# A two-layer cross-attention and FFN kernel: the second attention's slot reordered, so that maxima and scores of the next batch stand in one stretch

## The reference, cut to what matters

```python
q = (Q @ Wq_w + Wq_b).reshape(b, tq, 16, 8); k, v likewise from the context
scores = einsum('bhqd,bhkd->bhqk', q, k) / sqrt(8)
scores = where(mask == 0, -1e9, scores)
attn = softmax(scores, axis=-1)
out = einsum('bhqk,bhkd->bhqd', attn, v) @ Wo_w + Wo_b
x = x + out                      # the residual
```

## The kernel before, in words

| j = 0 | j = 1 |
|---|---|
| transposes of the next pair (L1884, L1886) | |
| scores(b), turn_out(b-1), folds(b) | scores(b), turn_out(b-1), folds(b) |
| out_projection(b-1), score_maxima(b+1) | out_projection(b-1), score_maxima(b+1) |
| ffn_turn (L1999), queries_keys (L1893, L1894) | values_rows (L1901, L1902) |
| values(b), ffn_project (L2006) | values(b), in every fourth slot four transposes for the last FFN (L395) |
| turn_maxima(b+1) | turn_maxima(b+1) |

## Time and profile before

### The profile page before, as it was taken

How to read it: one execution, slowest core, us unless ns; L and a number is a source line. 1 busy time by engine, 2 the same in 40 slices (tenths; PEclk the granted TensorE clock), 3 DMA queues, 4 the chain that set the end, 5 groups by cost and what they waited for, 6 DMA issues and landing times.

```text
span 716.7 us, 23519 instructions
## 1 busy us (share of the span) xinstructions
PE 680.4 (95%) x9268; PEld 569.8 (80%) x9273; DVE 556.9 (78%) x1635; ACT 388.7 (54%) x846; POOL 432.1 (60%) x558
## 2 busy tenths in 40 slices
PE   8999999999999999999999989999999999998875
PEld 6788888888888888889888878788888888875544
DVE  5887787697687698688687655787878887778996
ACT  2443553543544544445345444566766766766896
POOL 3597586487396388378477523455555646632775
PEclk9999999999999999999999999999999999998999
DMA  9511011101101101101100120000000000000011
GB/s 263 132 34 37 13 48 45 33 5 46 37 26 45 36 2 45 36 26 36 36 22 15 32 79 7 11 7 7 12 5 4 9 4 9 0 2 1 24 45 52
DMA packets 26766, 23.82 MB, mean 33 GB/s; under 512 B 7148, under 2 KB 23356, under 8 KB 26680
## 3 DMA queue, kind: packets, MB, share of 16 engines
q1 hardware_dynamic: 25864, 22.25, 11.1%
q10 hardware_dynamic: 816, 0.36, 0.2%
HBM read 10.25 MB, written 2.10 MB: 17 GB/s over the span
## 4 chain that ended last, share of the span: by engine, by line
PE 70%; DVE 17%; POOL 5%; issue 4%; ACT 3%; DMA 1%; SPq 0%; ACTq 0%; DVEq 0%
PE bank L1274 7%; PE bank L1316 6%; PE bank L1942 6%; PE bank L1172 5%; PE bank L1296 4%; PE bank L1975 4%; PE bank L1278 4%; PE bank L1307 3%; PE bank L1173 3%; PE bank L1174 3%; DVE a_am L911 3%; PE bank L1960 2%; DVE f_h_max L2192 2%; PE bank L1223 2%; PE bank L1232 2%
## 5 line engine op out<-in xcount | busy, mean ns | idle before, releaser
L741 POOL TENSOR_TENSOR a_turned<-a_turned,a_rope 128x512 f32<-128x512 f32 x63 | 81.7, 1297 | 55.7 <-DVE a_turned L848 55.7
L742 POOL TENSOR_TENSOR a_qr<-a_straight,a_turned 128x512 f32<-128x512 f32 x64 | 81.6, 1276 | 4.9
L845 DVE TENSOR_TENSOR a_straight<-bank,a_rope 128x512 f32<-128x512 f32 x63 | 43.0, 683 | 52.5 <-PE bank L1174 51.4
L1045 ACT CAST a_qb<-a_qr 128x512 bf16<-128x512 f32 x64 | 39.8, 622 | 65.9 <-POOL a_qr L742 65.9
L1296 PE MATMUL bank<-a_vs,a_probs 77*64 77x65 f32 x2048 | 66.8, 222 | 0.0
L1296 PEld LDWEIGHTS bank<-a_vs,a_probs 77*64 77x64 f32 x2048 | 62.6, 137 | 3.3
L753 POOL TENSOR_TENSOR a_k_turned<-a_k_turned,a_rope 128x308 f32<-128x308 f32 x61 | 48.4, 793 | 24.3 <-DVE a_k_turned L858 23.6
L1316 PE MATMUL bank<-a_wo,a_oTn 128*128 128x128 f32 x512 | 62.6, 275 | 0.2 <-ACT a_oTn L1073 0.2
L1316 PEld LDWEIGHTS bank<-a_wo,a_oTn 128*128 128x128 f32 x512 | 60.5, 192 | 1.2 <-ACT a_oTn L1073 0.5
L911 DVE TENSOR_REDUCE a_am<-bank 128x6 bf16<-128x462 f32 (+1 forms) x96 | 49.9, 576 | 12.1 <-PE bank L1232 12.0
L1274 PE MATMUL bank<-a_qr,a_kr 64*77 64x128 f32 x960 | 59.2, 273 | 0.0
(11 more groups left out here) (282 smaller groups left out, 1984.8 us busy)
## 6 DMA issues: line engine op xcount, KB each, us to landing
a_vs<-a_stage SPq DMA_DIRECT2D x16, 312.8 KB
out<-x_all SPq DMA_DIRECT2D x16, 128.0 KB, 1.8
x_all<-in_x_dram SPq DMA_DIRECT2D x7, 256.0 KB, 6.3
a_vs<-a_stage SPq DMA_DIRECT2D x4, 308.8 KB
a_mask_in<-in_mask SPq DMA_DIRECT2D x16, 77.0 KB, 5.7
a_wv<-in_ctx SPq DMA_DIRECT2D x16, 77.0 KB
a_ctx_in<-in_ctx SPq DMA_DIRECT2D x8, 128.0 KB
a_vs<-a_stage SPq DMA_DIRECT2D x4, 211.2 KB
```

The source lines that it names most:

```text
L741: steps.link(nc.gpsimd.tensor_tensor(tv, tv, rope[:, 1:2, :].broadcast_to([128, 4, S]), ALU.mult))
L742: nc.gpsimd.tensor_tensor(qr[P][:, 2 * k:2 * k + 2, :, :].rearrange("p t j s -> p (t j) s"), sv, tv, ALU.subtract if made else ALU.add).th ...
```

## The change

TensorE: scores(b+1) are made behind score_maxima(b+1) in the slot of b, ahead of values(b), instead of at the head of the next slot. Their ten matmuls are in a new order, with a wait in the middle on a new semaphore `rest_read`, which VectorE raises when it has reduced the rest of the maxima. values_rows stands ahead of the folds, turn_out behind them, queries_keys ahead of out_projection; out_projection is no longer inside score_maxima. ffn_turn and ffn_project go from j = 0 to the slot j = 1. VectorE: the rest is reduced first; the attention's statistics (j = 1) and start.rows (j = 0) go behind the residual, directly ahead of the maxima; normalised_rows goes behind the maxima. ScalarE: turned_out goes behind the exponentials of the first group, ffn_turned to j = 1 ahead of cast_keys.

```diff
@@ VectorE
         def maxima(b):
+            dve.wait_ge(x_full[2], b + 1)
+            nc.vector.tensor_reduce(max_r[:], pr[:, 0:256].rearrange("p (h k) -> p h k", k=RPAD), AX,
+                                    ALU.max).then_inc(rest_read, 1)
             for i in (1, 0):
                 dve.wait_ge(x_full[i], b + 1)
                 steps.did(nc.vector.tensor_reduce(max_m[:, 8 * i:8 * i + 8],
                                                   px[i][:].rearrange("p (h k) -> p h k", k=KM), AX, ALU.max))
-            dve.wait_ge(x_full[2], b + 1)
-            steps.link(nc.vector.tensor_reduce(max_r[:], pr[:, 0:256].rearrange("p (h k) -> p h k", k=RPAD), AX, ALU.max))
+            steps.wait()
+            dve.wait_ge(rest_read, b + 1)
             nc.vector.tensor_tensor(row_max, max_m[:], max_r[:], ALU.max).then_inc(maxima_ready, 1)
...
-            if j == 1 and more_pre(p):
-                ffn_residual(p + 2)
-                statistics(p + 2)
...
-            if j == 0 and more_pre(p):
-                start.rows(dve, steps, p + 2)
...
+            if j == 1 and more_pre(p):
+                ffn_residual(p + 2)
             if not first:
                 dve.wait_ge(bias_added, p + j)
                 residual(b - 1)
             if j == 1 and more_pre(p):
-                normalised_rows(p + 2)
+                statistics(p + 2)
+            if j == 0 and more_pre(p):
+                start.rows(dve, steps, p + 2)
             if turn(P, j, g, 1):
                 front.variances(steps)
             if j == 0 or more:
                 maxima(b + 1)
+            if j == 1 and more_pre(p):
+                normalised_rows(p + 2)
@@ ScalarE
             if j == 1 and more:
+                if more_pre(p):
+                    ffn_turned(p + 2)
                 cast_keys(p + 1, 1 - P, 0)
+            exps(b, (2,))
             if not first:
                 turned_out(b - 1)
-            exps(b)
+            exps(b, (0, 1))
             if j == 0:
-                if more_pre(p):
-                    ffn_turned(p + 2)
@@ TensorE
         def scores(b, P, j):
...
-            score(2, 0, 0, 4, True).then_inc(half_done, 1)
-            for i in range(3):
+            for i in range(2):
                 score(1, i, 1, i, i == 0)
                 score(0, i, 0, i, i == 0)
+            score(1, 2, 1, 2, False)
+            pe.wait_ge(rest_read, b + 1)
+            score(2, 0, 0, 4, True).then_inc(half_done, 1)
+            score(1, 3, 1, 3, False)
+            score(0, 2, 0, 2, False)
             pe.wait_ge(half_done, 2 * b + 2)
             score(2, 1, 1, 4, False)
             score(0, 3, 0, 3, False)
-            score(1, 3, 1, 3, False)
...
         turn_maxima(0)
+        scores(0, 0, 0)
         def slot(b, p, P, j, more, g, prev):
             if j == 0 and more:
                 transposes(p + 1, 1 - P)
-            scores(b, P, j)
-            if not first:
-                turn_out(b - 1)
-            folds(b)
-            score_maxima(b + 1, ...)        # out_projection(b - 1) inside; ffn_turn behind it for j == 0
+            if j == 1 and more:
+                if more_pre(p):
+                    ffn_turn(p + 2)
+                values_rows(p + 1)
+            folds(b)
+            if not first:
+                turn_out(b - 1)
             if j == 0 and more:
                 queries_keys(p + 1)
-            if j == 1 and more:
-                values_rows(p + 1)
+            if j == 1 and more_pre(p):
+                ffn_project(p + 2)
+            if not first:
+                out_projection(b - 1)
+            score_maxima(b + 1, ...)
+            scores(b + 1, ...)
             values(b, p, P, j)
             if back(P, j, prev):
                 front.rows(pe, prev, pm)
-            if j == 0 and more_pre(p):
-                ffn_project(p + 2)
             if j == 0 or more:
                 turn_maxima(b + 1)
```

More of the change, by code:

```diff
@@ L1475, in layer1_attention @@
     m_full, fold_ready, maxima_ready, half_done = sem("m_full"), sem("fold_ready"), sem("maxima_ready"), sem("half_done")
+    rest_read = sem("rest_read")
     vals_ready = sem("vals_ready")
@@ L1765, in slot @@
                 queries(p + 1, 1 - P)
-        pairs_loop(dve, slot, steps, 56)
+        pairs_loop(dve, slot, steps, 52)
         normalise(B - 1)
@@ L1806, in fold_in, with exps @@
             nc.scalar.copy(fold[CROW:FOLD, :], MAXIMA[CROW:FOLD, :]).then_inc(fold_ready, 1)
-        def exps(b):
-            for g in (2, 0, 1):
+        def exps(b, gs):
+            for g in gs:
                 act.wait_ge(s_full[g], b + 1)
@@ L1904, in values_rows, with score_maxima @@
             last.then_inc(values_full, 1)
-        def score_maxima(b, p, P, j, first):
+        def score_maxima(b, p, P, j):
             pe.wait_ge(maxima_ready, b)
-            if not first:
-                out_projection(b - 2)
             pe.wait_ge(s_free[2], b)
@@ L2033, in tensor @@
         pe.wait_ge(setup, 11)
-        score_maxima(0, 0, 0, 0, True)
+        score_maxima(0, 0, 0, 0)
         yield
         turn_maxima(0)
+        scores(0, 0, 0)
         def slot(b, p, P, j, more, g, prev):
@@ L2041, in slot @@
                 transposes(p + 1, 1 - P)
-            scores(b, P, j)
+            if j == 1 and more:
+                if pair(p, 1):
+                    pe.wait_ge(front.means_read, 1)
+                if more_pre(p):
+                    ffn_turn(p + 2)
+                values_rows(p + 1)
+            folds(b)
             if not first:
                 turn_out(b - 1)
-            folds(b)
[L2046 to L2053, removed]
-            if j == 0 and more_pre(p):
-                ffn_turn(p + 2)
             if j == 0 and more:
                 queries_keys(p + 1)
-            if j == 1 and more:
-                values_rows(p + 1)
+            if j == 1 and more_pre(p):
+                ffn_project(p + 2)
+            if not first:
+                out_projection(b - 1)
+            if j == 0:
+                score_maxima(b + 1, p, P, 1)
+                scores(b + 1, P, 1)
+            elif more:
+                score_maxima(b + 1, p + 1, 1 - P, 0)
+                scores(b + 1, 1 - P, 0)
             if pair(p, PAIRS - 1) and j == 0:
```

## The result

| | before | after |
|---|---|---|
| median of 4 runs, us | 718.45 | 729.23 (728.61 to 730.0) |
| ratio, 95% interval | | 1.0145 (1.0131 to 1.0159) |
| span of the profiled execution | 716.7 | 727.3 |

The change costs 10.6 us of span. The direction of the forecast was right, the size half: +5.2, 723.3, and the range ended at 729. The page's line of after answers to the earlier trace rows: TensorE is busy 5.1 us longer with the same work. Its records are longer than the steps between them, so a short wait stands inside busy time, and half of the 10.6 us doesn't show as idle time.

A forecast was written before the change was run, and what follows sets the result against it. TensorE's own program, busy 95% of the span, was taken as the bound. Loop turns +2.5, rows_in +3.9, prologue -0.9 and the last pairs -0.3 gave +5.2 us on 718.1, so 723.3, range 715 to 729.

The forecast's parts named there:

- T to T: One slot, between starts of turn_maxima: forecast 6.12 us (j = 0) or 6.83 (j = 1).
- The prologue's term: In the prologue scores(0) moves into TensorE's wait for normalised_rows(1): -0.9 us once.
- R to V: From TensorE's semaphore for the reduced rest to values: 0.86 us, three pairs of halves, one weight load and exit.
- T to O: From turn_maxima's start to out_projection's: 2.03 us (j = 0), 2.44 (j = 1).
- O to V: From out_projection's start to values': 1.90+0.86 us (j = 0), 2.20+0.86 (j = 1).
- The wait for the rest in mid-scores: New TensorE wait on VectorE amid the scores: about 0.5 us for j = 1, 0.1 to 0.3 for j = 0.
- R: TensorE's semaphore for the reduced rest: 1.90 us behind out_projection's start (j = 0), 2.20 (j = 1).
- rows_in: Folds wait for ScalarE's fold copy queued behind rows_in: 0.65 us in each of six slots, +3.9.
- the end's sum: Last two pairs: no statistics or start.rows, but turned_out is awaited; about -0.3 us.
- The rival that the changes of shape win: Three of seven tile-shape changes go per slot; without waits for the rest 707 us; chance 0.16.
- possible form of this rival: Semaphore 1.82 us behind out_projection's start everywhere, no exposed weight load: four slots 25.2 us, total 715.

The follow-up runs named there:

- x11: After without the attention's statistics in slots j = 1 (two bn_stats, memset, two bn_aggr left out): 725.01 us.
- x12: x9 with start.rows behind the maxima and, on POOL, ffn_bias behind spread_keys: 726.78 us.
- x3: After with four scores instead of five ahead of the wait on rest_read, and (2, 1) last: 730.51 us.
- x2: After with ScalarE's copy of the next batch's fold ahead of rows_in: 727.87 us.
- b3: Before with values_rows behind values for j = 1, and transposes behind turn_out for j = 0: 726.97 us.
- y2: Before with only values_rows moved behind values for j = 1: 730.34 us.
- y3: x9 without the attention's statistics and without 120 of 128 columns of start.rows: 724.3 us.
- y1: x9 with the wait on rest_read two scores later: 725.62 us.
- x8: x1 with, for j = 1, turn_out ahead of the folds and ScalarE's turned_out ahead of the exponentials: 724.8 us.
- x9: x8, x2 and x4 together: 724.05 us.
- x1: After with ffn_project ahead of the folds for j = 1, and VectorE's ffn_residual and statistics ahead of the residual: 732.95 us.
- x4: After with VectorE's front.gather at the end of its slot instead of ahead of the residual: 730.89 us.

## Why the prediction was right in direction and short in size

Growth of the stage in stretches of slots, forecast and measured, both from T to T:

| slots | forecast | measured |
|---|---|---|
| 0 to 3 | -0.54 | +1.2 |
| 4 to 7 | +0.36 | +0.5 |
| 8 to 11 | +0.36 | +1.2 |
| 12 to 27, four turns | 4 x 1.01 = +4.0 | 4 x 1.59 = +6.3 |
| 28 to the end | +1.0 | +1.35 |

The stage grew by 5.4 us more than forecast. The prologue's term is 1.6 of it, R to V 1.7, T to O about 1.1 and a late VectorE in slot 8 0.5, each told below; the rest is spread over the end.

**Right: what decides O to V.** The wait for the rest in mid-scores, late for j = 1 because of the statistics, is shown by x11. R for j = 1 was forecast at O+2.2 and came at O+2.26 (the (2, 0) record at 513.92), for j = 0 at O+1.80 where 1.90 stood. O to V for j = 0 is 2.76 as summed, by luck: the 0.10 here makes up for the 0.10 that the next step missed. x12 shows that for j = 0 it is the floor and not start.rows, which the forecast blamed for 0.08.

**Mis-sized: R to V, 0.86.** It took one exposed load of weights. The half_done wait in the same stretch has a second: (2, 0) and (2, 1) use different halves of the array and one bank, and the second waits for the first (in x3, with four scores between them, R to V is 0.96 too). R to V is 0.96 to 0.97, inside the bounds of 0 and 0.2 that stood there for one load; that there are two was not counted. The 14 slots j = 1 have O to V 3.11 to 3.22 instead of 3.06, 1.7 us together.

**Mis-sized: T to O.** 2.03 to 2.09 against 2.03 for plain j = 0, 2.72 against 2.68 behind rows_in (together about 0.5 us), 2.41 against 2.44 for j = 1, but 2.58 in four slots with L395, 0.6 us. Those four are the slots behind a held combination: `queries` end 0.34 behind T there, and values_rows, which wait for them, start at T+0.44 instead of T+0.33. The sum had no term for GpSimd holding up VectorE.

**Right, for the wrong price: rows_in.** Forecast T to O 2.68, measured 2.72. But as a cause it was overvalued: x2 takes the wait away and gets 1.4 us of the 3.9, since the copies behind it on ScalarE were the next bound. Two prices for one delay don't add up, and the last interval of a slot (7.18 to 6.52) alone gave 0.66.

**Wrong: the prologue, -0.9.** scores(0) did move into the hole ahead of L1884; the folds stand 2.03 behind the first turn_maxima instead of 2.78 before. But slot 0 then makes scores(1) as well, and its length stays 7.52 (7.56 before). The sum took both the filled hole and the steady slot's saving of the scores at its head, for the same 1.3 us; they come back only behind the last turn_maxima, where no scores are left. This is the largest miss: the sum had slot 0 shorter by 0.76 (a steady slot j = 0) and 0.9, and it is shorter by 0.04, which is 1.6 of the 1.8 us missed in slots 0 to 3. Slot 1 is long (7.35 against 6.90 of slot 3), but was so before (6.33 against 5.94). Left out of the end's sum, that return hid what its waits cost: from 653.88 on, TensorE waits 1.01 and 0.35 for the folds' copy and 0.35 for out_projection each time, as nothing covers them there.

**Missed: VectorE late for another reason.** Slot 8 took 6.66 and not 6.12. front.row_maxima (L367, 0.67 us) stands at the end of VectorE's slot before, the gather and three row steps behind it, so the residual starts 505.76, O+0.99 instead of O+0.59, and O to V is 3.15. Only start.rows was counted for j = 0. In the later turns this lateness lies under the rows_in wait.

**The rival that the changes of shape win** fell where the prediction put its weak point. By the Trainium skill, TensorEngine Tiling (Array Packing), section Key Properties, a change of tiling mode drains the array. The change does take some out of each slot, and b3 and y2 measure what one is worth, 0.10 to 0.15 in the slot j = 1. Against it stand 0.28 per slot (2.76 less the 2.48 without a wait), which y3 shows to be there with VectorE ready at once, and y1 with the wait satisfied. In x8 a pair that is neither held up nor behind rows_in (slots 14 and 15) takes 6.17+7.03 = 13.20 against 6.89+6.44 = 13.33, so there the reordering gains 0.13; held up (slots 22 and 23) it takes 13.60. The pair behind rows_in takes 6.62+6.56 = 13.18 in x9 against 6.78+5.88 = 12.66. These pairs, the first slots and the end make the 0.7%. How it splits was worked out from traces only; no run takes it apart. The prediction's possible form of this rival has a slip: its terms give 25.0 for four slots, not 25.2, and so 714, not 715.

## What to carry to other kernels

Where one engine is busy all the time, a reordering that brings a producer, its reader on another engine and the next writer of the same bank into one stretch has a floor: last matmul's end, reduction, semaphore, reload. Work it out before the savings, and look for what each moved piece was covering, since three of the edits here lost to exactly that (ffn_project in x1, values_rows in y2, the transposes in b3). Look at the other engines too when VectorE's work changes place: one small instruction that comes a moment behind a long one of GpSimd costs as much as the waits that the edits were made for, and an edit's gain can be lost to it (x4, y3). In a sum by steady slots, check the first and the last slot by counting the pieces in them: the same work may be credited twice.

## What the runs showed of the hardware

A wait of TensorE in a stretch of half-row matmuls costs more than the time until the semaphore: the first record behind it took 0.373 us instead of 0.272 and the next pair came 0.1 later, even when the wait itself was short; where the semaphore had come before (y1, the wait on rest_read) the records ran on in pairs without a gap. fp32 records of unpaired halves follow each other at 0.11 us, just as pairs do, so an unpaired half costs as much as a pair. The granted clock of TensorE fell from 1.00 to 0.50 (the lower of its two levels, 1.2 GHz) for 3.4 us in the end of the stage in x3 and x4, behind waits of 1.0, 0.35 and 0.35 us, and stayed 1.00 in after with the same waits; it was worth 1.2 us in one interval (8.37 against 7.18), so a difference of that size in one of these kernels is no finding about its edit. VectorE's TENSOR_TENSOR of 128x16 from `max_m` and `max_r` took 0.17 to 0.18 us where nothing held it and up to 1.08 us where a TENSOR_TENSOR of GpSimd stood ahead of it, ending 0.03 us behind that one; the reductions from banks kept their 0.42 and 0.68 us beside the same work of GpSimd. A wait inside a pipelined group shows in no list of waits; the step from the first record to the next group (1.32, 1.61 or 1.97 us for the same 20 records) is what gives it away.
